# Sharing out the PSUM banks anew in a fused attention and expert block: three score banks and a ring of three, in place of two and four

## What is computed

```
q, k, v = (h @ Wq + bq), (h @ Wk + bk), (h @ Wv + bv)      # q and k rotated
logits  = einsum('bqhgd,bkhd->bhgqk', q, k) / 8, causal
w       = softmax(logits)
out     = einsum('bhgqk,bkhd->bqhgd', w, v) @ Wo + bo
```

## Time and profile before

| | |
|---|---|
| median of 3 runs | 1347.31 us (1346.81 to 1349.45) |
| the profiled execution, its own time | 1347.43 us |
| its span, first to last instruction | 1345.6 us |
| mean granted TensorE clock | 0.979 of full speed |
| busy: PE, weight loads, DVE, ACT, POOL | 1267.9, 814.4, 903.1, 563.5, 548.2 us |

### The profile page before, as it was taken

The page is one execution under the profiler, slowest core; times in us unless marked ns, Lnnn a source line. Parts: engine busy times, 40 slices in busy tenths (PEclk is TensorE's granted clock), DMA queues, the critical chain, the costliest instruction groups (busy, mean ns, idle before and its releaser), DMA issues.

```text
span 1345.6 us, 18461 instructions
## 1 busy us (share of the span) xinstructions
PE 1267.9 (94%) x6732; PEld 814.4 (61%) x6732; DVE 903.1 (67%) x1775; ACT 563.5 (42%) x1178; POOL 548.2 (41%) x599
## 2 busy tenths in 40 slices
PE   2689999999999999999999999999995899999998
PEld 1446555545655554565555456565544688888887
DVE  3757878777787867778786777977738444444443
ACT  2445535454454545455454544544442223222322
POOL 2644466463456626345663544655224011110100
PEclk9699999999999999999999999999996899999999
DMA  5000000000000000000000000000001000000001
GB/s 137 1 0 1 1 1 1 1 1 1 1 1 1 1 1 1 1 1 0 1 1 1 1 1 0 1 0 1 1 1 47 0 24 24 23 23 23 23 1 32
DMA packets 18445, 12.94 MB, mean 10 GB/s; under 512 B 7104, under 2 KB 15680, under 8 KB 18368
## 3 DMA queue, kind: packets, MB, share of 16 engines
q1 hardware_dynamic: 11072, 9.58, 2.4%
q10 hardware_dynamic: 7296, 2.36, 0.7%
HBM read 10.88 MB, written 1.05 MB: 9 GB/s over the span
## 4 chain that ended last, share of the span: by engine, by line
PE 83%; DVE 10%; ACT 2%; POOL 2%; issue 1%; ACTq 1%; DVEq 0%; POOLq 0%
PE PS L1023 18%; PE PS L1071 13%; PE PS L977 11%; PE PS L1005 10%; PE PS L1085 8%; PE PS L1007 8%; PE PS L953 2%; PE PS L1042 2%; DVE part_max L762 2%; PE PS L990 2%; PE PS L960 2%; PE PS L1033 2%; DVE full L778 2%; PE PS L980 1%; PE PS L1010 1%
## 5 line engine op out<-in xcount | busy, mean ns | idle before, releaser
L762 DVE TENSOR_REDUCE part_max<-PS 128x1 f32<-128x512 f32 (+2 forms) x576 | 340.0, 618 | 132.4 <-PE PS L977 110.1
L599 ACT ACTIVATE full<-PS 128x512 f32<-128x512 f32 x384 | 223.4, 599 | 198.3 <-PE PS L1007 185.7
L1005 PE MATMUL PS<-QT,KT 128*128 128x512 f32 (+3 forms) x640 | 272.0, 425 | 5.9 <-ACT diag L608 2.4
L977 PE MATMUL PS<-KT,QT 128*128 128x512 f32 (+3 forms) x640 | 248.9, 415 | 3.1 <-DVE V L743 2.1
L1007 PE MATMUL PS<-QMT,KT 128*128 128x512 f32 (+3 forms) x640 | 233.3, 365 | 0.0
L468 POOL TENSOR_TENSOR full<-full 128x512 f32<-128x512 f32 x128 | 164.4, 1315 | 155.9 <-PE PS L1023 154.8
L977 PEld LDWEIGHTS PS<-KT,QT 128*128 128x128 f32 x640 | 118.7, 191 | 139.1 <-DVE part_max L762 62.3
L608 ACT ACTIVATE diag<-PS 128x512 f32<-128x512 f32 (+3 forms) x256 | 111.3, 441 | 214.9 <-PE PS L1010 185.1
L1023 PE MATMUL PS<-full,V 128*64 128x512 f32 x768 | 190.0, 605 | 0.0
L872 DVE TENSOR_TENSOR full<-full,PS 128x512 f32<-128x512 f32 x128 | 87.9, 688 | 145.5 <-ACT full L648 145.5
L496 POOL TENSOR_TENSOR rot_cos<-qkv_sb,cos_sb 128x320 f32<-128x320 f32 x64 | 60.4, 943 | 277.3 <-DVE qkv_sb L740 275.0
(11 more groups left out here) (109 smaller groups left out, 1662.1 us busy)
## 6 DMA issues: line engine op xcount, KB each, us to landing
full<-in_L_ffn_experts_w_dram SPq DMA_DIRECT2D x24, 256.0 KB, 3.1
out_dram<-XA SPq DMA_DIRECT2D x4, 256.0 KB, 2.3
wqkv<-in_L_attn_Wq_dram ACTq DMA_DIRECT2D x1, 512.0 KB, 4.4
bqkv<-in_L_attn_bq_dram ACTq DMA_DIRECT2D x1, 512.0 KB, 9.6
wo_sb<-in_L_attn_Wo_dram SPq DMA_DIRECT2D x1, 512.0 KB, 8.8
sin_sb<-in_k_sin_dram ACTq DMA_DIRECT2D x1, 512.0 KB, 8.9
full<-in_L_wmod_dram SPq DMA_DIRECT2D x1, 384.0 KB, 9.4
cos_sb<-in_k_cos_dram ACTq DMA_DIRECT2D x1, 256.0 KB, 9.7
```

What stands on the lines that cost most here:

```text
L599: nc.scalar.activation(full[:, k % QUADS, r, :], PS[:, bank, :], ACT.Exp).then_inc(probs_ready, 1)
L762: nc.vector.reduce_max(part_max[:, t, b:b + 1], PS[:, bank, 0:width], AX.X).then_inc(ring_dve, 1)
L977: last = nc.tensor.matmul(PS[:, bank, 0:w], QT[:, ch % 2, h, t * P:(t + 1) * P], KT[:, 0, keys:keys + w], start=True, stop=not last_bank)
L1005: nc.tensor.matmul(o, KT[:, 0, keys:keys + P], QT[:, ch % 2, h, q0:BANK], start=True, stop=False)
```

## The change

Two constants: three score banks in place of two, and a ring of three in place of four. The ring starts at bank 3. No instruction is added or taken away, and the list of steps stays.

```diff
-    SCORE_BANKS, RING_BANKS, KEY_SLOTS = 2, 4, 5
+    SCORE_BANKS, RING_BANKS, KEY_SLOTS = 3, 3, 5
...
-        SCORES, RING, AV = 0, 2, 6
+        SCORES, RING, AV = 0, 3, 6
```

## The result

| | before | changed |
|---|---|---|
| median | 1347.88 us (4 runs, 1346.81 to 1349.45) | 1368.95 us (4 runs, 1368.82 to 1369.21) |
| profiled execution, time and span | 1347.43 and 1345.6 us | 1369.21 and 1367.3 us |
| ratio to before | | 1.0156 (95% interval 1.0138 to 1.0173) |

The change makes the kernel 21.1 us slower; +18 was forecast, and 1368.95 lies in the forecast's own range of 1356 to 1380.

What follows compares the result with a forecast made beforehand. The prediction took the PE to set the pace; +28 for the ring and -10 for the scores made +18 on 1347.4, so 1365.4 us, own range 1356 to 1380, stretched to 1350 to 1391.

Steps and rivals of the forecast that it cites:

- The ring with one bank less: Attention stage: weight loads wait for the read three slots back, not four; +28 us, bounds +26 and +46.5.
- The net sum by runs: Longest shortage of each of 68 DVE backlogs, 46.5 us, less what the PE idles there already: 32.2 us.
- the 4 us taken off for prefetched loads: Deduction from 32.2 us, since a weight load ahead of its matmul can be slightly late unnoticed; 6.3 us at most.
- The third score bank: Attention scores: a score step may start once the exponential three steps back is done; -10 us, bounds -16.7 and 0.
- the count under the upper bound: Score loads held by ACT: 58 with 19.4 us, of which 48 with 16.7 us lie outside the ring's backlog runs.
- Moved waits at 0: 220 PE waits move from score steps to `pv` steps; priced at 0, or 11 us if each cost 0.05 more.
- Why the ring is short: At bursts of maxima, DVE takes 0.686 us for a bank the PE fills in 0.23; additions also delay reductions.
- The score wait was what mattered: Rival: the 50.9 us of waits named before score loads are real, so the kernel gets faster, 1325 us; chance 0.10.
- The delay is absorbed: Rival: 15 to 20 us of lag vanish in other PE waits, such as `maxed` before `qmax`; within 3 us of 1347; chance 0.10.
- Shortages don't share: Rival: DVE's backlog moves with the PE, each run costs its full longest shortage, +46.5; 1384 us; chance 0.17.
- The clock drops: Rival: more stalls lower the PE clock in attention, to a mean of 0.95; +49 us, 1396 or 1414 us; chance 0.03.
- The repeat of a group: Time after which the key/value groups' pattern recurs in attention; to grow from 239.5 to some 243 or 244 us.

Runs made afterwards that it cites:

- the ring alone: Against the kernel before: ring cut from four banks to three, score banks kept at two, bank 2 used by nothing; 1378.54 us, ratio 1.0225.

## Why the prediction was right, point by point

- *The ring with one bank less, +28 (bounds +26 and +46.5).* Shown: +31.0 by the ring alone. The net sum by runs, 32.2, was within 1.2 us; the 4 us taken off for prefetched loads brought it further away, and nothing here shows them. Nearly all that the forecast of the whole was short by lies here.
- *The third score bank, -10 (bounds -16.7 and 0).* Shown as the difference between the ring alone and the changed kernel: -9.6 us. It was measured with the ring of three only; what it is worth beside a ring of four would need a ninth bank, and wasn't tried. The sum came within 0.4 us partly by luck: 10 was picked between 8.9 and 16.7, and the count under the upper bound missed 3.0 us of held loads.
- *Moved waits at 0.* Shown by the traces: the loader's idleness before those 220 `pv` is 30.7 us with the waits and 30.7 without.
- *Why the ring is short.* The prediction named DVE's backlog, out of additions and the mismatch between a reduction of 0.686 us and a fill of 0.23. The case read out in full hung on an addition, and that led me to expect too much of them: they carry 6 us, the reductions about 18 of 31 (if the third score bank keeps its worth), and ACT's copies, which the prediction didn't name, stand behind half of the idleness that remains.
- *The score wait was what mattered.* It fell: removing 19.0 us of held loads (21.5 by the ring alone, 2.45 in the changed kernel) returned 9.6 us, and of the 50.9 us of the table much was named "issue" as soon as no bank could be blamed.
- *The delay is absorbed.* It fell: the waits for `maxed` went only from 10.4 to 8.7 us, and the lag grows in every group.
- *Shortages don't share.* It fell for one bank less (+31, not +46.5), and was the nearer one for two banks less (+135 against 125).
- *The clock drops.* It fell for this change: 1.00 in the window from 400 to 650 us, and 0.98 from 60 to 150 us, as before. With a ring of two it did drop, to 0.84 from 60 to 150 us. What the Trainium skill tells of PSUM-queue cycling (TensorE: Matmul & The Clock Gate, section on psum-queue depth-cycling) doesn't appear in the changed kernel; whether it is what the ring of two shows, no run tells.
- *The repeat of a group,* forecast at 243 or 244 us, is 245.4. The forecast of the whole was nearer than that of the part, since the last pair step gives back 2.9 us once.

The rule of repeating gaps from the Trainium skill (Perfetto Trace Analysis, Identifying Performance Opportunities, under Optimization Strategy) found both pools about equally short, 18.8 against 19.4 us by the prediction's count, and taken alone would have made the change worth nothing. Measured, a bank is worth 31 us to the ring and 9.6 to the scores.

## What to carry to other kernels

To price a buffer less, lay each use's start against the release one buffer further back, over the whole trace; add up only the longest shortage of each backlog, less what the engine idles in it anyway. That sum held to 1.2 us for one bank, and was 23% too low for two, so here it was good for one step only. And if two classes of work share banks, look at where in the schedule each is short: a split that changes with the stage beat both fixed ones (1339.7 us against 1347.0 and 1369.0).

## What the runs showed of the hardware

A held weight load starts 0.05 us after the release, or 0.11 in some cases, in every kernel here. Held loads that a pool of banks removed (10.4 us) returned under 2 us, so idle loading isn't time one for one: at 513.83 the loader had idled 0.72 us and the array 0.28. The granted clock isn't the same in every execution ahead of pair step 2: 1.00, 0.91 and 0.83 from 80 to 100 us in three kernels that differ by less than 1% in time, and it fell to 0.50 from 60 to 80 us in the ring of two.
